# Two adapter layers on one core: sums moved behind the gated copies on VectorE, gated products set into the middle of a product on TensorE

## The reference

```python
x = x + einsum('bnr,bor->bno', einsum('bni,bri->bnr', x, B0[ids]), A0[ids])      # layer 0
base   = x @ W.T                                                                 # layer 1
logits = x @ Wr.T + 5.0 * one_hot(lang)
gates  = softmax over the top 2 of logits, placed in E = 8 columns
h      = einsum('btd,erd->bter', x, A)
x = x + base + 2.0 * einsum('bter,bte,eor->bto', h, gates, B)
```

## Time and profile before

| what | value |
|---|---|
| median of 3 runs | 530.76 us |
| the profiled execution | 533.64 us, span 531.8 us |
| TensorE busy | 511.5 us (96%) |
| VectorE / ScalarE / POOL busy | 390.7 / 274.4 / 278.1 us |
| one pair (12 of them) | 30.0 us |
| mean granted clock of TensorE | 0.987 of 2.4 GHz |

### The profile page before, as it was taken

How to read it: one execution, slowest core, us unless ns; L and a number is a source line. 1 busy time by engine, 2 the same in 40 slices (tenths; PEclk the granted TensorE clock), 3 DMA queues, 4 the chain that set the end, 5 groups by cost and what they waited for, 6 DMA issues and landing times.

```text
span 531.8 us, 9808 instructions
## 1 busy us (share of the span) xinstructions
PE 511.5 (96%) x3356; PEld 462.6 (87%) x3356; DVE 390.7 (73%) x908; ACT 274.4 (52%) x617; POOL 278.1 (52%) x259
## 2 busy tenths in 40 slices
PE   7799979979999999999999999999999999999996
PEld 6688979879889879898999999898999999898996
DVE  5769695686684988777786878878786977878712
ACT  4555423622554655655566465655656465555621
POOL 5432386858848574536535564536536563545120
PEclk9699999999999999999999999999999999999999
DMA  8932434304443132442516142442615142340201
GB/s 328 318 106 82 130 90 128 110 20 129 129 102 118 40 107 113 112 148 67 191 41 178 61 138 101 108 149 64 195 41 170 63 137 108 108 150 1 81 28 53
DMA packets 31159, 60.45 MB, mean 114 GB/s; under 512 B 4349, under 2 KB 20477, under 8 KB 31109
## 3 DMA queue, kind: packets, MB, share of 16 engines
q1 hardware_dynamic: 24432, 38.81, 22.7%
q0 software_dynamic: 6656, 20.98, 13.7%
q10 hardware_dynamic: 20, 0.03, 0.0%
HBM read 43.02 MB, written 16.78 MB: 112 GB/s over the span
## 4 chain that ended last, share of the span: by engine, by line
PE 83%; DVE 9%; issue 3%; ACT 2%; DMA 1%; POOL 1%; DVEq 0%; ACTq 0%; POOLq 0%
PE o_bank L732 24%; PE x_bank L741 16%; PE o_bank L695 12%; PE o_bank L741 11%; PE o_bank L708 6%; PE x_bank L614 5%; PE b_bank L590 3%; PE o_bank L684 2%; PE x_bank L708 2%; DMA a_in<-in_L_cond_A_dram,a_run 1%; DVE xs L1189 1%; DVE bx_all L1340 1%; DVE a_raw L1312 1%; PE x_bank L575 1%; DVE bx_own L1342 1%
## 5 line engine op out<-in xcount | busy, mean ns | idle before, releaser
L732 PE MATMUL o_bank<-w_hi,xs 128*128 128x512 f32 x384 | 125.9, 399 | 0.3 <-ACT out_sb L1045 0.2
L531 POOL TENSOR_TENSOR xs<-xt,xs 128x512 fp32r<-128x512 f32 x36 | 47.0, 1308 | 97.2 <-ACT xs L997 50.2
L695 PE MATMUL o_bank<-w_hi,xs 128*128 128x324 f32 (+1 forms) x336 | 91.5, 347 | 0.0
L732 PEld LDWEIGHTS o_bank<-w_hi,xs 128*128 128x128 f32 x384 | 72.1, 188 | 18.3 <-issue 2.0
L542 POOL TENSOR_TENSOR a_t<-a_raw,a_t 64x1024 fp32r<-64x1024 f32 x22 | 52.9, 2403 | 45.1 <-DVE bx_t L1347 44.1
L732 PE MATMUL o_bank<-w_lo,xs 128*128 128x512 f32 x192 | 75.4, 393 | 0.0
L400 POOL DMA_INDIRECT a_in<-in_L_cond_A_dram,a_run x64 | 60.7, 948 | 19.3 <-issue 19.2
L1312 DVE STREAM_TRANSPOSE a_raw<-a_in 128x1024 f32<-128x1024 f32 x32 | 64.5, 2021 | 2.5 <-DMA a_in<-in_L_cond_A_dram,a_run 2.5
L695 PEld LDWEIGHTS o_bank<-w_hi,xs 128*128 128x128 f32 x336 | 60.6, 191 | 5.6 <-issue 1.0
L1232 DVE STREAM_TRANSPOSE xt<-x_near 128x512 f32<-128x512 f32 x48 | 57.6, 1204 | 0.5 <-issue 0.5
L695 PE MATMUL o_bank<-w_lo,xs 128*128 128x324 f32 (+1 forms) x168 | 57.4, 342 | 0.0
(11 more groups left out here) (155 smaller groups left out, 1106.5 us busy)
## 6 DMA issues: line engine op xcount, KB each, us to landing
out_dram<-out_sb SPq DMA_DIRECT2D x30, 512.0 KB, 3.4
x_near<-in_x_dram SPq DMA_DIRECT2D x104, 128.0 KB, 3.0
w_in<-in_L_cond_W_dram SPq DMA_DIRECT2D x6, 512.0 KB, 8.3
x_far<-in_x_dram SPq DMA_DIRECT2D x16, 128.0 KB, 3.7
x_near<-in_x_dram SPq DMA_DIRECT2D x2, 512.0 KB, 3.2
out_sb<-in_L_cond_W_dram SPq DMA_DIRECT2D x2, 512.0 KB, 15.6
a_in<-in_L_cond_A_dram,a_run POOLq DMA_INDIRECT x64, 3.5
out_dram<-out_sb SPq DMA_DIRECT2D x4, 162.0 KB, 2.6
```

The lines of the kernel that those rows point to most:

```text
L531: nc.gpsimd.tensor_tensor(xs[:, slot, 1, :, :], raw, xs[:, slot, 0, :, :].bitcast(F32), ALU.subtract).then_inc(ss_lo, 1)
L695: mm = pe.matmul(O[part][:, 0:hi - lo], x1_at(n, c // CB, low)[:, c % CB, :], w[:, c, lo:hi], start=(k == 0), stop=(k == K3 - 1), skip_gro ...
L732: mm = pe.matmul(O[0][:, 0:hi - lo], xs[:, raw_slot(j, c // CB), low, c % CB, :], w[:, c, lo:hi], start=(k == 0), stop=(k == K3 - 1), skip ...
```

## The change

1. VectorE, tiles 2, 4 and 6: `bx_rest` of the second of the two tiles moves from before `x1_lo_part` to behind `gated_t_part`. (In the odd tiles both lists leave nothing for this loop.)
2. t4's copies: ScalarE's `t_last_split` moves from pair 0 to tile 7, ahead of its `out_part`, with a new wait on `w12_read`, which TensorE signals when the first 12 matmuls of part 2 of tile 7 have read the weights that t4 replaces. VectorE's `t4_lo` moves to the end of tile 7. In pair 0 `aT_part(a + 2)` moves ahead of the gates, as in the other pairs.
3. TensorE, every pair: the seventh product is cut in 6 and 6 matmuls, and the three `pair_lora(b, ...)` stand between them.

```diff
-            def product(slot, hi_at, lo_at, bank_out, start):
-                for k in range(3 * CB):
+            def product(slot, hi_at, lo_at, bank_out, start, first=0, end=3 * CB):
+                for k in range(first, end):
...
-                mm.then_inc(p_psum, 1)
+                if end == 3 * CB:
+                    mm.then_inc(p_psum, 1)
...
-                make_part(n, 2, 0, 12)
+                mm = make_part(n, 2, 0, 3 * CB)
+                if n == K - 1:
+                    mm.then_inc(w12_read, 1)
...
-                product(s4_slot(q), *w_block(1, 1), PC, False)
+                product(s4_slot(q), *w_block(1, 1), PC, False, 0, 6)
                 pe.wait_ge(gt_ready, 2 * (b + 1))
                 pair_lora(b, 0, O[0])
                 pair_lora(b, 1, PB)
                 pair_lora(b, 2, PD)
+                product(s4_slot(q), *w_block(1, 1), PC, False, 6)
                 pair_lora(a, 2, PC)
...
             def t_last_split(c):
+                act.wait_ge(w12_read, 1)
...
                 if n == K - 1:
                     split_a(K)
                     put_part(K + 1)
+                    for c in range(CB):
+                        t_last_split(c)
...
-                if q == 0:
-                    for c in range(CB):
-                        t_last_split(c)
...
                 weigh_experts(n)
-                for m in bx_tiles(n)[len(ahead):]:
-                    bx_rest(m)
                 if n + 1 < K:
                     x1_lo_part(n + 1)
...
                 gated_t_part(n)
+                for m in bx_tiles(n)[len(ahead):]:
+                    bx_rest(m)
...
+                if n == K - 1:
+                    for c in range(CB):
+                        t4_lo(c)
...
-                if q == 0:
-                    for c in range(CB):
-                        t4_lo(c)
-                if more and q > 0:
+                if more:
                     aT_part(a + 2)
                 choose_experts(a)
                 weigh_experts(a)
-                if q == 0:
-                    aT_part(a + 2)
```

More of the change, by code:

```diff
@@ L173, in two_adapter_layers @@
         t_step, t_hi, t_lo, f_hi, f_lo = map(sem, ("t_step", "t_hi", "t_lo", "f_hi", "f_lo"))
-        f_lo4 = sem("f_lo4")
+        f_lo4, w12_read = sem("f_lo4"), sem("w12_read")
         p_psum, so_psum, ab_copied, bc_copied, cd_copied, s7_copied = map(
@@ L830, in _ @@
                 add_lora(n, 1)
-                make_part(n, 2, 12, K3)
+                make_part(n, 2, 3 * CB, K3)
                 add_lora(n, 2)
```

## The result

The changed kernel takes 526.52 us (median of 20 runs, 522.91 to 529.78), the kernel before 533.46 us in the same session (20 runs, 527.75 to 536.33): a ratio of 0.989, 95% interval 0.9865 to 0.9915, so 1.1% faster. The forecast was 528.5 us and a gain of 2.3 us; the gain is 5.9 us by this ratio and 6.9 us by the two medians. The profiled execution took 527.15 us, its span 525.4 us against 531.8.

The account below looks back on a forecast made before the run. TensorE, busy in 96% of the span, was taken as the bound. Waits gave 4.7 us, less 1.1, plus 0.2, less 1.5 for one low clock: 2.3 off 530.76 gave 528.5 us, range 525.2 to 531.3.

Parts of the forecast that it names:

- The waits for `gt_lo`: TensorE's four waits for VectorE's second gated copy, 8.0 us in tiles 2, 4, 6 and pair 0, would go.
- two came back at the output bank: First matmuls of tiles 3 and 5 would wait 2.6 and about 3 us for ScalarE's output copy; gains 1.7 and 0.15.
- a low clock: TensorE's clock was expected to drop behind one of the two moved waits, costing 1.5 us; chance 0.50.
- tile 6's: The 1.40 us wait in tile 6 would really go, with 0.1 us of restart: gain 1.5 us.
- The rival that no wait comes back: Tiles 3 and 5: the output bank would be free in time, giving 521.3 us; chance 0.10.
- the start: Time of the kernel before from which the gain was taken: the median shown, 530.76 us.
- The short waits of pair 0: Of 1.3 us in three short waits in the first pair, 0.5 us was counted as gained.
- a permutation of a full stretch ends when it ended before: VectorE in tile 2: reordered work would reach the transposes `xT` of tile n+3 no earlier than before.
- the lower side: Tile 2, VectorE: moved `bx_rest` could shorten by up to 2.2 us outside POOL's work; not used in the sum.
- The split: Seventh product of every pair, cut in 6 and 6: cost 0.09 us a pair, 1.1 us over 12 pairs.
- The rival that it outweighs the rest: Every pair: `gt_hi` starts late and TensorE stops in each of twelve products; 532.2 us at 0.4 a pair; chance 0.08.
- The tail: End of the kernel, last copy and four last stores: gain 0.2 us, bounds 0 and 0.9.

Follow-up runs that it names:

- the kernels with the B sums last: Changed kernel, `bx_rest` behind the transposes' copies: product cut in 7 and 5, ratio 1.0244; whole, 0.9747; whole with GpSimd's gathers behind the gated sums, 0.9757 and 0.9182.
- the B sums alone: Kernel before with only `bx_rest` of tiles 2, 4 and 6 moved behind the gated copies: 563.32 us, ratio 0.9915.
- the whole product: Changed kernel with its seventh product left whole, 12 matmuls ahead of the gated sums: 561.53 us, ratio 0.9883.
- the split at three: Changed kernel with the seventh product cut in 3 and 9 matmuls instead of 6 and 6: 592.55 us in one run.
- gathers held back: Changed kernel with GpSimd's six gathers of a pair issued only once the gated sums of both tiles are ready: 527.92 us, ratio 0.9871.
- t4's move: Kernel before with only t4's copies moved to tile 7 and the transpose of A ahead of the gates in pair 0: 566.02 us, ratio 0.9993.
- the split alone: Kernel before with only the seventh product cut in 6 and 6, run twice: 589.43 us, ratio 1.037; 588.68 us, ratio 1.0422.

## Why the prediction was right, and where it was short

**The mechanism held.** The waits for `gt_lo` went, two came back at the output bank at tiles 3 and 5, 0.5 to 0.6 us shorter than said (2.10 and 2.40 us; said 2.6 and about 3), one was followed by a low clock, tile 6's went for good. The pairs take 30.07 us as said; the twelve short waits behind that are too short to be listed. The rival that no wait comes back is refuted by the two rows, and the kernels with the B sums last show what it would have been worth: 6.5 to 6.6 us on the ruler.

**The gain was mis-sized, and the time was close partly by luck.** The terms add up to 5.8 us where 2.35 was said; all but the low clock (-1.6, said -1.5) came out on the better side. The time was only 2.0 us under the forecast because the start was too low as well: it was taken from a median of 3 runs, 530.76 us, and 20 runs give 533.46. Between medians the gain was 4.6 us more than forecast, and 2.7 of that were made up by the start.

**The short waits of pair 0 were the largest miss.** The step "of the 1.3 us of shorter waits I count 0.5 as gained: they hang on POOL's and ScalarE's chains as much as on VectorE's" failed. Its first reading was off too: the stretch from 200 us that it calls the first pair is pair 1, and pair 0, from 166.34 to 199.60, had idle time to give. Five waits stood there (0.82, 0.21, 0.45, 0.50, 0.36), 2.34 us in all, of which the prediction's list lacked the one of 0.21; the pair took 33.26 us, 3.26 above a full one. So each wait cost 0.18 us on average beside its own length, not 0.1, at the full clock throughout. One of 0.31 us is left, and the pair takes 30.59: 2.7 us were gained where 0.9 + 0.5 were said. They hung on t4's copies and the transpose that made room for them: the run with that move alone loses the first three in its first 21 us, that with the B sums alone keeps them all, the one of 0.21 us for ScalarE's copy included (0.29 there). Whether VectorE's `w_lo` operations or ScalarE's `t_last_split` did it no run parts.

**VectorE's stretch got shorter, which the sum excluded.** The sentence "a permutation of a full stretch ends when it ended before" failed by 0.5 us in each of tiles 2 and 4. `bx_all` at 73.06 took 0.28 us and was in just ahead of GpSimd's next instruction, at 73.08; the three behind it took 0.85 to 0.99 beside GpSimd's row of operations of 0.88 us. Before, all four were that long. This is the rule that was cited for the lower side, the Trainium skill, SBUF — State Buffer, on the two separate sides: the pair of ports goes to whichever engine starts first, for its whole instruction. By it up to 2.2 us were to be had (2.4 by the quiet rows of tile 2, where the four take 1.27 us); 0.56 of it came, in either tile, and tiles 3 and 5 start 0.5 us earlier for it.

**The split** cost 0.07 us a pair where 0.09 was said. The rival that it outweighs the rest, given 0.08 and a threshold of 0.28 us a pair, is false on the chip of the result and true on every slow one. The reason given against it, that VectorE sits idle ahead of `gt_hi` so that nothing delays it, holds for VectorE and left out the hand-off.

**The tail** was worth 0.9 and not 0.2 us, the upper bound. The second tile's parts are copied earlier, so that three of the four stores are issued 1.1 us and more ahead of the last, before 0.4 us and more; the last one landed 2.2 us after its issue, before 3.0.

**The low clock.** One stretch was said and one came, but that is one profile. Behind the same two waits there was a low stretch after the first alone (the result and its repeat on a slow chip, the whole product, the split at three), after both (gathers held back), after neither (B sums alone). Behind the waits of 2.67 and 3.05 to 3.09 us it came after the first alone (the kernel before, t4's move) or after both (the two runs of the split alone). The spans of the 20 runs group at 521, 525 and 528 us with falling clock, and the sixteen runs of the kernels that do not wait there lie within 2.8 us of each other (519.03 to 521.83), where the changed one's twenty lie within 6.9. That fits the Trainium skill, TensorE: Matmul & The Clock Gate, Part 1, by which the moment depends on where a free-running watch lies. How many stretches the groups hold was not measured.

## What to carry over

When a wait sits behind a producer that is full to the last microsecond, reordering its queue moves the wait to the next consumer; look for what stands behind it on every queue (here `xT`, then ScalarE's output copy) and move the filler behind all of them. An idle TensorE cost its restart (0.18 us) here and, behind waits of 2.1 us and more, at times a low clock, 1.5 us and more (behind the 1.40 and 0.82 us of the kernel before there was none), so removing the last wait is worth more than shortening it. And matmuls between a hand-off and its use are cover even where one chip's profile shows that six would do: on another chip the same hand-off took fourteen times as long, and the sign of the change turned.

## What was not expected of the hardware

Chips differ in a hand-off from TensorE to VectorE and ScalarE while GpSimd issues six gathers: 0.3 us on the two chips of the fast kind, 4.3 to 4.5 us in pairs 1 to 9 on the two slow ones with a trace of it, with operations and packets as long as elsewhere; the kernel before takes 533 us on the former and 564 to 568 on the latter. In the pairs without gathers, and with the gathers 1.4 us behind `gt_hi` (242.13 to 243.51), the difference was gone.
